# Filler matrix products before the first transpositions of each couple, in a two-layer attention and mixture-of-experts kernel

## The reference

```python
q_l = _landmarks(q, nL)          # 64 landmarks, each a mean of 16 queries
k_l = _landmarks(k, nL)
L = softmax(einsum('bhtd,bhld->bhtl', q, k_l))
P = _iterative_inv(softmax(einsum('bhld,bhmd->bhlm', q_l, k_l)))
N = softmax(einsum('bhld,bhtd->bhlt', q_l, k))   # 64 landmarks x 1024 keys, per head
y = L @ (P @ (N @ v))
```

## Time and profile before

| | |
|---|---|
| median of 3 runs | 1485.21 us |
| profiled execution: its own time | 1496.12 us |
| profiled execution: span | 1494.4 us |
| granted clock, mean of the span | 0.921 of full speed |
| PE busy | 1287.5 us (86%), 10705 instructions |
| VectorE (DVE) busy | 1028.4 us (69%) |
| ScalarE (ACT) busy | 879.3 us (59%) |

### The profile page before, as it was taken

One profiled execution on the slowest core, in us unless ns is written; L12 is line 12 of the kernel. 1 busy time (PEld: TensorE's weight loads), 2 busy tenths in 40 slices (PEclk: granted clock), 3 DMA queues, 4 the chain that ended last, 5 costly groups with the idle time before them and its releaser, 6 DMA issues. The chain is left out here.

```text
span 1494.4 us, 26939 instructions
## 1 busy us (share of the span) xinstructions
PE 1287.5 (86%) x10705; PEld 613.7 (41%) x10705; DVE 1028.4 (69%) x1283; ACT 879.3 (59%) x1518; POOL 245.4 (16%) x303
## 2 busy tenths in 40 slices
PE   3876999999999999999999788888997787699950
PEld 2651222222222222222222355545996555477840
DVE  3758998898998889899996456645544788511206
ACT  1541888888878878888888545542231566444314
POOL 4110110000000000000000111004431222145442
PEclk9995999999999999999999878767997799899985
DMA  3564033332233432112200111000000111323205
GB/s 78 178 213 106 14 79 79 69 77 59 53 92 94 118 88 63 36 34 58 63 10 8 49 31 43 15 14 2 23 30 22 35 34 33 84 77 107 78 30 168
DMA packets 78473, 94.93 MB, mean 64 GB/s; under 512 B 13428, under 2 KB 48972, under 8 KB 77316
## 3 DMA queue, kind: packets, MB, share of 16 engines
q1 hardware_dynamic: 73260, 83.12, 21.5%
q0 software_dynamic: 5088, 10.09, 2.2%
HBM read 54.27 MB, written 38.50 MB: 62 GB/s over the span
## 5 line engine op out<-in xcount | busy, mean ns | idle before, releaser
L585 DVE TENSOR_REDUCE b_mx<-psum 128x2 f32<-128x1024 f32 x512 | 601.2, 1218 | 68.9 <-PE psum L666 67.8
L643 ACT ACTIVATE b_exp_ring<-psum 128x512 f32<-128x512 f32 x1024 | 555.6, 600 | 156.7 <-PE psum L702 153.5
L702 PE MATMUL psum<-b_q,b_k 75*128 75x512 bf16 x1024 | 311.4, 386 | 5.3 <-DMA b_q<-b_neg 3.8
L678 PE MATMUL psum<-b_exp_ring,b_v 128*32 128x512 f32 x2048 | 273.6, 606 | 0.9 <-ACT b_exp_ring L643 0.7
L702 PEld LDWEIGHTS psum<-b_q,b_k 75*128 75x128 bf16 x1024 | 79.2, 97 | 321.5 <-ACT b_exp_ring L643 222.0
L664 PE MATMUL psum<-b_k,b_q 64*128 64x512 bf16 x512 | 169.6, 396 | 26.3 <-DVE b_mx L585 13.2
L666 PE MATMUL psum<-b_ko,b_qo 64*128 64x512 bf16 x512 | 169.7, 396 | 0.0
L717 POOL CAST b_neg<-b_neg_rest 16x128 bf16<-16x128 f32 x32 | 8.9, 280 | 660.0 <-DVE b_neg_rest L596 660.0
L664 PEld LDWEIGHTS psum<-b_k,b_q 64*128 64x128 bf16 x512 | 44.3, 93 | 129.5 <-DVE b_mx L585 47.6
L1737 ACT ACTIVATE e_hT<-psum,e_b 128x358 f32<-128x358 f32 (+1 forms) x96 | 53.5, 559 | 73.7 <-issue 57.2
L1222 POOL DMA_INDIRECT x_disp<-x_norm,row_sent x64 | 62.8, 981 | 149.4 <-PE psum L1562 101.1
(11 more groups left out here) (271 smaller groups left out, 1557.7 us busy)
## 6 DMA issues: line engine op xcount, KB each, us to landing
b_q<-q_ops SPq DMA_DIRECT2D x48, 192.0 KB
b_k<-k_ops SPq DMA_DIRECT2D x48, 192.0 KB
k_ops<-a_k SPq DMA_DIRECT2D x20, 256.0 KB, 3.2
x_disp<-b_zeros SPq DMA_DIRECT2D x13, 320.0 KB
e_x<-x_disp SPq DMA_DIRECT2D x8, 516.0 KB
v_ops<-a_vs SPq DMA_DIRECT2D x4, 1024.0 KB, 5.1
b_v<-v_ops SPq DMA_DIRECT2D x16, 256.0 KB
av_out<-b_acc SPq DMA_DIRECT2D x128, 32.0 KB, 1.7
```

Of the source, the lines that this page charges most:

```text
L585: nc.vector.reduce_max(mx[:, d % 2, :, i // 2, i % 2], pair, AX.X).then_inc(sem("b_max_done"), 1)
L643: act.activation(ex[:, n % E_RING, :], g.bank(5 + n % 3), ACT.Exp, scale=ATT_SCALE)\
L678: last = nc.tensor.matmul(AV[32 * i:32 * i + 32, :], v[s][:, at_v:at_v + 32], ex[:, (4 * group + i) % E_RING, :], start=(kb == 0), stop=(k ...
L702: nc.tensor.matmul(g.bank(5 + n % 3), k[s][0:XROWS, h, kb * P:(kb + 1) * P], q[s][0:XROWS, h, half * BANK:(half + 1) * BANK], start=True, ...
```

## The change

`transposed` gets a filler. For the couples c = 1, 2, 3 and s = 0, PE waits for the copy-out as before, then multiplies 768 columns of the transposed tokens (`c_xT`) with the query weights into D0, as one product of 512 and one of 256 columns, and only then waits for the exponential. The 8 transpositions that follow overwrite the result, and nothing reads it. For s = 1 and for c = 0 only the order of two waits changes.

```diff
+                def busy(columns):
+
+                    lo = 0
+                    while lo < columns:
+                        n = min(BANK, columns - lo)
+                        nc.tensor.matmul(D0[:, 0:n], g.wqkv1[:, 0:P], xT[:, 0:n], start=True, stop=True)
+                        lo += n
+
                 def transposed(c, s):
                     k = PAIRS * b + 2 * c + s
-                    pe.wait_ge(sem("c_en"), k + 1)
                     if c:
                         pe.wait_ge(sem("c_enT"), k - 1)
-                    else:
+                        if s == 0:
+                            busy(3 * BANK // 2)
+                    pe.wait_ge(sem("c_en"), k + 1)
+                    if c == 0:
                         pe.wait_ge(sem("c_v"), 2 * (b + 1))
                         if s and b + 1 < B:
                             pe.wait_ge(sem("c_t1"), b + 2 - EARLY)
```

## The result

The changed kernel takes 1469.33 us (median of 4 runs, 1467.9 to 1471.41), beside 1488.13 us for the kernel before (median of 4, 1483.02 to 1492.66): 18.8 us less, a ratio of 0.988 with a 95% interval of 0.985 to 0.991. The forecast was 1464 in a range of 1456 to 1480.

The account below looks back on a forecast made before the run. TensorE's half clock in the second layer's landmark softmax, lost at idle gaps, was taken as the bound. Batches 0 to 2 win 15.5 us, batch 3 5.9: 21.4 off the 1485.2 median gives 1464 us, range 1456 to 1480.

Parts of the forecast that it names:

- The bound and the mechanism: Second layer's landmark softmax: TensorE's clock falls with idle gaps in its couples; filling them wins 21.4 us.
- The price of a filler: Before first transpositions: 0 at full clock (1.33 us in a 1.59 us gap), about 1.9 us later at half clock.
- Couples of batches 0 to 2: First transpositions of couple 0 to couple 3: 17.19 us at full clock, gains 5.08, 1.31 and 5.11 us.
- The ends: Couple 3's first transpositions to next batch's input, batches 0 to 2: 7.93 us each, gains 0.77, 2.35, 0.84.
- the third rival: Clock held, then falls at batch ends or in later stages: 6 to 11 us lost, 1470 to 1475; chance 0.12.
- Batch 3: Starts slow, full clock by couple 1's transpositions: couples 21.7 us (gain 3.2), end 8.00 (gain 2.7), together 5.9.
- From the profile to the median: The stage's 21.4 us, read from the profiled execution, taken unchanged off the median run, 1485.2, giving 1463.8 us.
- The first (batch 3 does not come back): Transpositions around batch 3's filler do not lift the clock: gain only 9.8 us, time 1475; chance 0.13.
- The second (the filler is paid and does not hold the clock): In the couples, slow fillers cost 1.9 us each: seven make 13.3, time 1498, at worst 1518; chance 0.10.
- The fourth: Change does nothing, as the median run lacks the profiled run's half-clock stretches: 1482 to 1487 us; chance 0.05.
- the ring: One couple's first transpositions to the next's, through scores, maxima and exponential: 5.73 us at full clock, 8.31 at half.

## Why the prediction was right

**The bound and the mechanism.** Right. The stage won 20.0 us against 21.4 forecast, and the run without a filler takes the time of the kernel before. Of the 20.0 us, 14.7 are in the couples and 5.3 in the ends.

**The price of a filler.** 0 at full clock: right, with 0.30 us left over and 0.26 forecast. The 1.33 us for 768 columns were a little high: 1536 columns took 2.57. At half clock 1.9 was forecast. The filler before couple 3 alone ran wholly at half clock in batch 2 and delayed the first transpositions by 4.32 - 2.78 = 1.5 us; the 32-row one cost 2.05.

**Couples of batches 0 to 2.** Forecast 17.19 us each; measured 17.88, 17.20, 17.20, a gain of 4.39 + 1.30 + 5.10 = 10.8 and not 11.5. The 0.7 missing is in batch 0: VectorE was held up there, which the prediction did not have (last section).

**The ends.** Forecast 7.93 us each; measured 9.54, 7.84, 7.85. In batch 0 the third rival came true on a small scale, 1.7 us:

```profile
876.50 1.09 PE L1156 MATMUL psum<-ident,c_en 128*128 128x128 f32 x8 [1.05 <-ACT c_en L1078]
878.55 1.09 PE L1156 MATMUL psum<-ident,c_en 128*128 128x128 f32 x8 [0.95 <-ACT c_enT L1070]
...
880.76 5.35 PE L1182 MATMUL psum<-c_enT,c_vl 128*32 128x256 f32 x64 [0.51 <-ACT c_enT L1070]
886.04 1.09 PE L1105 MATMUL psum<-ident,x_norm 128*128 128x128 f32 x8
```

The clock fell by 881 us, behind gaps of 1.05, 0.95 and 0.51 us, and the weighted sum took 5.35 us. The long first gap is not needed for it: the second profile of the change fell at the same place of batch 2 behind 0.30, 0.95 and 0.51 us, and not in batch 0 behind 0.84, 0.95 and 0.51. The three ends won -0.84 + 2.44 + 0.92 = 2.5 us, where 4.0 were forecast. Of the four profiles of the changed kernel, with and without batch 3's extra filler, three have one such fall. What decides which end falls is open. With the ends filled the one profile had none, but so had one of the four without.

**Batch 3.** Forecast 21.7 us for the couples and 8.00 for the end, measured 20.90 and 7.92, a gain of 6.7 and not 5.9: the clock was back during the filler, and I had taken it as back only behind the filler. 10.8 + 2.5 + 6.7 = 20.0. That it came back at all rested on one row of the kernel before and had a rival of 0.13; the run with fillers in batch 3 alone bears it out. Where the clock goes down there was not foreseen and varies: with the filler doubled and with a filler before couple 3 alone the first transpositions behind the wait of 2.55 us still took 1.10 and 1.09 us, and the second ones 1.97.

**From the profile to the median.** The measured time is 5.5 us above the forecast's 1463.8: 2.6 because the gain was 18.8 and not 21.4, and 2.9 because the kernel before has a median of 1488.13 us with its fourth run, and 1485.2 was used. The two spans differ by 25.9 us, of which the stage is 20.0. Another 5.0 lie in the iterative inverse behind it, which took 1136.45 - 1026.01 = 110.4 us before and 1112.4 - 1006.9 = 105.5 after. That is not the filler: the run without one had 104.9 there, three with one in the same set 104.8 to 105.9, and the seven profiles of the other two sets, all with fillers, 110.5 to 112.2. What parts the two groups, chip or something else, is open; on which chip the first two profiles were taken is not on record. The sum made from stage rows alone was the right one to take off a median; the difference of two spans would have said too much. What the timed runs lack of the stage's 20.0, 1.2 us, is inside the interval (13.5 to 22 us).

**The rivals.** The first (batch 3 does not come back) was real for a 32-row filler only. The second (the filler is paid and does not hold the clock) was seen nowhere but there, in batch 3; its sum of seven slow fillers left out couple 3 of batch 1, which ran slow too, so by its own terms it should have been eight, 15.2 us. The third took 1.7 us of one batch, against 6 to 11 forecast for it. The fourth falls with the timed runs. What in the profile spoke best for the forecast was batch 1 of the kernel before, two whole gaps passed without a fall: the run with 256 columns shows that a good part of the gap was enough.

## What to carry to other kernels

Where an engine idles for a moment in a ring that it bounds itself, and its clock falls there, read the ring at either clock first: 8.31 against 5.73 us held most of the prize, 14.7 of 20.0 us here. Useless work that fits into the gap cost nothing while the clock was up. It need not close the gap (256 columns did), and what does not fit is paid on the ring (0.67 us each with 1536 columns). Only 128-row work also brought a lost clock back here, so check what a filler costs where the clock is already down. Then read the gain from the touched stage: the two spans differed by 5.0 us more in a stage that the change does not touch.

## What the runs showed of the hardware

Transpositions held and restored TensorE's clock as 128-row products did (stage 145.0 against 144.9 us); 32-row products held it in the couples, and did not bring it back in over 30 us (in that profile the granted clock is 0.50 from 983 to 1014 us, with PE never idle up to 1010).

A longer wait came from VectorE in batch 0. The timeline of GpSimd and VectorE there, and VectorE's same operation in batch 1:

```profile
869.24 2.37 POOL L1023 TENSOR_TENSOR c_oT<-c_num,c_den 128x1024 f32<-128x1024 f32 x1 [13.61 <-DMA c_den<-recs]
...
869.77 2.92 DVE L938 TENSOR_TENSOR c_xc<-x_res,c_small 128x1024 f32<-128x1024 f32 x1
```

```profile
909.93 1.22 DVE L938 TENSOR_TENSOR c_xc<-x_res,c_small 128x1024 f32<-128x1024 f32 x1
```

GpSimd multiplies from 869.24 to 871.61 us, both inputs in SBUF. VectorE's subtraction (L938) is issued at 869.77 and takes 2.92 us instead of 1.22; it ends 1.08 us behind GpSimd's end, as if it had begun only then. That held back the maxima and so couple 3 by 0.7 us (idle 1.05 us and not 0.29 before its first transpositions). The distance is 1.07 or 1.08 us in the ten other profiles in which the two meet, wherever in GpSimd's instruction the subtraction was issued. In the kernel before the two did not meet:

```profile
868.22 2.36 POOL L1023 TENSOR_TENSOR c_oT<-c_num,c_den 128x1024 f32<-128x1024 f32 x1 [13.49 <-DMA c_den<-recs]
...
871.44 1.22 DVE L938 TENSOR_TENSOR c_xc<-x_res,c_small 128x1024 f32<-128x1024 f32 x1
```

GpSimd's multiplication was over at 868.22 + 2.36 = 870.58 us, and the subtraction began at 871.44. The Trainium skill (SBUF — State Buffer, Who interferes with whom) says that a VectorE operation with two SBUF inputs and a GpSimd operation that reads SBUF exclude each other for a whole instruction; this trace agrees, with 2.92 against 1.22 us. Whether the 0.7 us come back when GpSimd's multiplication is moved out of the way was not tried.
